# Attention 0: the product of the values with the ratio of the smoothing scales made by VectorE instead of GpSimd

## The reference, cut to what matters

```python
v = _fp8_linear_pertensor(ln_out, wv, wv_scale, v_in_scale).reshape(b, s, g, d)
core = _gqa(q, k, v).reshape(b, s, nh * d)
...
xout = _gqa(qx, kx, vx).reshape(b, s, nh * d)
cat = jnp.concatenate([core, xout], axis=-1)
catq = _div_clamp_fp8(cat, proj_smooth)
return jnp.einsum('bsi,oi->bso', catq, wproj) * (proj_in_scale * proj_w_scale)
```

## Time and profile before

| | before |
|---|---|
| median of 3 runs | 1577.19 us |
| profiled execution | 1575.72 us, span 1574.0 us |
| TensorE busy | 1366.4 us (87%) |
| VectorE busy | 1215.8 us (77%) |
| ScalarE busy | 1018.8 us (65%) |
| GpSimd busy | 853.1 us (54%) |
| mean granted TensorE clock | 0.957 |

### The profile page before, as it was taken

How to read it: one execution, slowest core, us unless ns; L and a number is a source line. 1 busy time by engine, 2 the same in 40 slices (tenths; PEclk the granted TensorE clock), 3 DMA queues, 4 the chain that set the end, 5 groups by cost and what they waited for, 6 DMA issues and landing times. The chain is left out here.

```text
span 1574.0 us, 30371 instructions
## 1 busy us (share of the span) xinstructions
PE 1366.4 (87%) x11712; PEld 1173.5 (75%) x11712; DVE 1215.8 (77%) x2318; ACT 1018.8 (65%) x2168; POOL 853.1 (54%) x912
## 2 busy tenths in 40 slices
PE   0356999999999999999999996999769898994995
PEld 0356899999999999999999985676536555553995
DVE  7999888888888888888888797633448988886554
ACT  4687677877777777778777774312136665652773
POOL 2688767667677676676775464101114433341673
PEclk9999999999999999999999998999979998995997
DMA  3100000000100000001001002340254002003563
GB/s 102 37 24 28 15 22 15 15 21 15 35 15 14 22 15 15 22 15 35 3 14 51 2 1 78 77 62 21 57 97 74 15 1 68 1 15 132 182 216 127
DMA packets 62239, 69.85 MB, mean 44 GB/s; under 512 B 5424, under 2 KB 54800, under 8 KB 61968
## 3 DMA queue, kind: packets, MB, share of 16 engines
q1 hardware_dynamic: 59488, 60.54, 14.6%
q0 software_dynamic: 2432, 7.34, 1.4%
q10 hardware_dynamic: 176, 0.04, 0.0%
HBM read 55.56 MB, written 12.34 MB: 43 GB/s over the span
## 5 line engine op out<-in xcount | busy, mean ns | idle before, releaser
L903 POOL TENSOR_TENSOR RB<-YS,M 128x512 bf16<-128x512 f32 x128 | 151.8, 1186 | 180.3 <-DVE YS L753 180.3
L579 ACT ACTIVATE QT<-B,sm 128x256 f32<-128x256 f32 x256 | 130.4, 560 | 163.8 <-PE B L435 163.8
L1769 POOL TENSOR_SCALAR_AFFINE_SELECT P<-P 128x1024 f32<-128x1024 f32 x64 | 82.1, 1282 | 154.7 <-ACT P L1623 154.7
L455 PE MATMUL SS<-QT,KT 128*128 128x256 f32 x512 | 154.8, 397 | 11.4 <-DVE mx L714 11.3
L892 POOL TENSOR_TENSOR yy<-vv,half 128x12 f32<-128x12 f32 x64 | 147.8, 2310 | 5.3
L403 PE MATMUL PA<-WH,XQ 128*128 128x256 f32 x512 | 140.2, 305 | 7.0 <-ACT SQ L608 7.0
L733 DVE TENSOR_TENSOR QN<-QN,yy 128x512 f32<-128x512 f32 x128 | 134.1, 1048 | 1.7 <-POOL yy L892 1.5
L714 DVE TENSOR_REDUCE mx<-SS 128x4 bf16<-128x512 f32 x128 | 88.2, 689 | 60.7 <-PE SS L447 59.7
L405 PE MATMUL PA<-WL,XQ 128*128 128x256 f32 x512 | 128.8, 283 | 0.0
L726 DVE TENSOR_REDUCE vv<-SQ 128x6 f32<-128x768 f32 x128 | 120.6, 942 | 0.0
L435 PE MATMUL B<-identf,QN 128*128 128x128 f32 x768 | 105.5, 274 | 6.4 <-ACT LNT L534 6.4
(11 more groups left out here) (331 smaller groups left out, 4516.1 us busy)
## 6 DMA issues: line engine op xcount, KB each, us to landing
W<-in_w SPq DMA_DIRECT2D x16, 1024.0 KB
Q<-qsc SPq DMA_DIRECT2D x48, 128.0 KB
WR<-in_wprojT SPq DMA_DIRECT2D x16, 256.0 KB, 3.0
K<-ksc SPq DMA_DIRECT2D x12, 256.0 KB
qsc<-T POOLq DMA_DIRECT2D x8, 384.0 KB, 4.2
X<-in_x SPq DMA_DIRECT2D x4, 512.0 KB, 5.9
CR<-in_xctxT SPq DMA_DIRECT2D x8, 256.0 KB, 2.8
RSM<-rsm_d SPq DMA_DIRECT2D x16, 128.0 KB, 4.1
```

Source lines behind the costliest of these rows:

```text
L455: pe.matmul(SS[:, 256 * z:256 * z + 256], k[:, 128 * z:128 * z + 128], q[:, 256 * z:256 * z + 256], start=True, stop=False)
L579: a.activation(QT[i % 2][:, o:o + 256], B1[:, o:o + 256], ACT.Identity, bias=col(n + "b"), scale=col(n + "w"))
L903: p.tensor_tensor(RB[i % 2][:], YS[:], M[:], ALU.subtract).then_inc(s_rb, 1)
```

## The change

The function `pool_values_scaled` goes, and `dve_values_scaled` takes its place, with the same operands and the same two waits. In VectorE's step it stands behind the quantisation of the output, and it is for unit `n - 2`, where GpSimd had made unit `n - 3` between the quantised inputs and `RB`.

```diff
--- before.py
+++ after.py
@@ -733,6 +733,12 @@
             v.tensor_tensor(q[:, 0:4], q[:, 0:4], y[:, 6 * h:6 * h + 4].unsqueeze(2).broadcast_to([128, 4, 128]),
                             ALU.mult).then_inc(s_mul, 1)
 
+        def dve_values_scaled(v, i):
+            v.wait_ge(s_vev, i + 1)
+            if i >= 4:
+                v.wait_ge(s_LO, i - 3)
+            v.tensor_tensor(VR1[i % 4][:, :, 0:128], V[i % 7][:, :, 0:128], RSM[i // NB % 2][:, 1], ALU.mult).then_inc(s_vq, 1)
+
         def dve_quant(v, i):
             o = PO[:, :, 0:258].rearrange("p z (j d) -> p z j d", d=129)
             v.wait_ge(s_LO, i + 1)
@@ -806,6 +812,8 @@
                     dve_quad_round(v, q4, k + 1)
                 if 0 <= n - 6 < N:
                     dve_quant(v, n - 6)
+                if 0 <= n - 2 < N:
+                    dve_values_scaled(v, n - 2)
                 for at_, g in weight_steps(n):
                     if at_ == W_CENTRE0 or at_ == W_CENTRE1:
                         dve_weights_centre(v, g, at_ == W_CENTRE1)
@@ -890,13 +898,6 @@
                 p.tensor_scalar(v_, v_, 1.0 / 128, EPS, ALU.mult, ALU.add).then_inc(*ps.up())
                 p.wait_ge(*ps.at())
                 p.tensor_tensor(yy[j % 2][:], v_, half[:], ALU.pow).then_inc(s_rstd, 1)
-
-        def pool_values_scaled(p, i):
-            g = i // NB
-            p.wait_ge(s_vev, i + 1)
-            if i >= 4:
-                p.wait_ge(s_LO, i - 3)
-            p.tensor_tensor(VR1[i % 4][:, :, 0:128], V[i % 7][:, :, 0:128], RSM[g % 2][:, 1], ALU.mult).then_inc(s_vq, 1)
 
         def pool_rounded(p, i):
             p.wait_ge(s_ys, i + 1)
@@ -930,8 +931,6 @@
                     q4, k = quad_at(n)
                     pool_quad_round(p, q4, k)
                     pool_quad_round(p, q4, k + 1)
-                if 0 <= n - 3 < N:
-                    pool_values_scaled(p, n - 3)
                 if 0 <= n - 6 < N:
                     pool_rounded(p, n - 6)
                 for at_, g in weight_steps(n):
```

## The result

| | before | changed |
|---|---|---|
| median of device time, us (16 runs each) | 1579.86 | 1572.56 |
| profiled execution: time, us | 1575.72 | 1573.67 |
| profiled execution: span, us | 1574.0 | 1571.9 |
| GpSimd busy, us (instructions) | 853.1 (912) | 776.6 (784) |
| VectorE busy, us (instructions) | 1215.8 (2318) | 1233.5 (2446) |

The ratio of the medians of paired series is 0.9949 (95% interval 0.9934 to 0.9964); of 1577.2 us that is -8.05 us, between -10.4 and -5.7. Forecast were 1569.2 us and -8.0. The median itself is 3.4 us above 1569.2, because the three runs that the forecast started from have a median of 1577.19 us and these 16 one of 1579.86; the plain difference of the two medians is -7.3 us.

What follows compares the result with a forecast made beforehand. TensorE was taken to bound the kernel from 170 to 930 us, VectorE from 80 to 170. Terms -6.4 - 1.2 - 0.4 = -8.0 us gave 1569.2 from a median of 1577.19; range 1564.0 to 1577.0.

Steps and rivals of the forecast that it cites:

- Rival B: 170 to 930 us: RB's stalls stay, waiting for something unseen; only 1.6 us gained elsewhere, 1575.6 us; chance 0.05.
- the forecast 0.44: Stalled steps: RB, started earlier, meets less of QN's product and takes 1.16 instead of 1.60 us.
- The steady term: 170 to 930 us: TensorE's six stalls for RB go, 6.4 us gained, between 4.2 and 6.6.
- 0.37 still fits: Weight-means steps: VectorE's added product costs 0.37 us and fits the 0.66 us before TensorE wants mx.
- The ceiling of 6.6: 170 to 930 us: most that could be gained, all six of TensorE's stalls for RB removed.
- The first stretch: 80 to 170 us, VectorE busy: products cost 2.6, relief 3.1 and 0.7; net -1.2 us, between +2.9 and -3.8.
- The -0.7 us for QN's product at 95.28: First stretch: without VR delaying GpSimd's reciprocal root, QN's product no longer waits 0.67 us.
- The last steps: End of the attention: RB wait of 1.07 goes, two products ahead of mx cost 0.7; net -0.4 us, -1 to +0.5.
- What was to be seen: Signs of being right: no RB waits from 170 to 930 us, VR 0.41 us before RB, GpSimd down 95, VectorE up 45.
- rival C: Each step: RB starts first and VectorE's product waits 1.16 us for it; 1612 us, slower; chance 0.09.
- the 0.3 named: 170 to 930 us: VectorE's idle time before mx was to fall by about 0.3 us a step.
- New waits for mx: Sign of being wrong: TensorE newly waits for mx after 170 us; cover gone would cost up to 5.7 us.

Runs made afterwards that it cites:

- the three profiles: The changed kernel profiled three times, each beside the kernel before; the ratios to it were 0.9949, 0.9953 and 0.9950.
- the doubled product: The changed kernel with each VR made twice on VectorE; ratio 1.0267 to the kernel before, 42 us slower.

## Why the prediction was right, and where its terms were not

**Direction and mechanism: right.** RB stood behind VR in GpSimd's queue, and that was the stall of the six steps. Rival B is refuted by every kernel that takes VR from in front of RB: the stalls went. GpSimd's side of the formerly stalled step in the changed kernel, with the DMA issue of SP, VectorE's product for QN and TensorE's restart:

```profile
461.66 0.40 POOL L879 CAST W<-WR 128x256 bf16<-128x256 f32 x1
...
462.08 0.34 SPq L321 DMA_DIRECT2D WR<-in_wqT  x1
...
466.42 4.31 POOL L853 TENSOR_SCALAR WR<-WR,csc 128x256 f32<-128x256 f32 x4 [1.79 <-DMA WR<-in_wvT]
...
470.99 2.30 POOL L900 TENSOR_TENSOR yy<-vv,half 128x12 f32<-128x12 f32 x1
473.25 1.15 POOL L904 TENSOR_TENSOR RB<-YS,M 128x512 bf16<-128x512 f32 x1
...
473.32 1.63 DVE L733 TENSOR_TENSOR QN<-QN,yy 128x512 f32<-128x512 f32 x1 [0.33 <-POOL yy L900]
...
474.46 0.40 PE L479 MATMUL PC<-identb,RB 128*128 128x128 bf16 x4 [0.16 <-POOL RB L904]
```

Against the earlier trace rows, the last cast, the loads and the scaling come as a block; the interval from the last cast to the start of the scaling is 4.76 us, 4.85 before. The prediction had RB start 0.69 us earlier. Measured from the point at which TensorE would have gone on without a wait (480.11 before, 474.30 here), RB started 0.62 us ahead of it before and 1.05 now: 0.43 gained. The scaling starts 0.45 us earlier against that point but takes 4.31 us instead of 3.61, so it ends 0.25 later, and that is taken from VR's 0.69. RB itself takes 1.15 instead of 1.60 us, 0.45 for the forecast 0.44. Together 0.88 against a stall of 1.03: 0.16 stays, six times. The step that failed is that an earlier start leaves the scaling's length alone.

**The steady term: 6.4 forecast, 4.5 by the listed waits, 2.8 to 3.2 in TensorE's time.** 5.6 of the 6.6 went, and 1.1 came back as listed waits for mx. But the time between the restarts, at like clock and without the 0.69 of the last mx, fell by 3.1, 2.8 and 3.2 us only in the three profiles. The step that failed is "0.37 still fits", in the step with weight means. VectorE and TensorE there in the changed kernel:

```profile
479.21 0.82 PE L435 MATMUL B<-identf,QN 128*128 128x128 f32 x6
479.47 0.68 DVE L714 TENSOR_REDUCE mx<-SS 128x4 bf16<-128x512 f32 x1
...
480.20 0.70 PE L455 MATMUL SS<-QT,KT 128*128 128x256 f32 x2 [0.18 <-DVE mx L714]
480.74 0.28 PE L458 MATMUL SS<-negib,mx 128*128 128x128 bf16 x2
```

mx ends at 480.15 and TensorE goes on at 480.20. I had read the slack as 0.66 us in the step of the earlier trace rows and called it the tighter one. The other weight-means step, the one right behind the stall, reads in the kernel before:

```profile
484.91 0.68 DVE L714 TENSOR_REDUCE mx<-SS 128x4 bf16<-128x512 f32 x1
...
485.88 0.82 PE L435 MATMUL B<-identf,QN 128*128 128x128 f32 x6
486.54 0.60 PE L455 MATMUL SS<-QT,KT 128*128 128x256 f32 x2
486.97 0.28 PE L458 MATMUL SS<-negib,mx 128*128 128x128 bf16 x2
```

That is 486.54 - 485.59 = 0.95 us of slack, and it looks wider; but TensorE comes there 1.03 us late because of the very stall that the change removes. The kernel with VR behind RB on GpSimd, without stall and without a product on VectorE, shows what is really there:

```profile
483.81 0.82 PE L435 MATMUL B<-identf,QN 128*128 128x128 f32 x6
483.94 0.68 DVE L714 TENSOR_REDUCE mx<-SS 128x4 bf16<-128x512 f32 x1
...
484.67 0.70 PE L455 MATMUL SS<-QT,KT 128*128 128x256 f32 x2
485.21 0.28 PE L458 MATMUL SS<-negib,mx 128*128 128x128 bf16 x2
```

TensorE goes on 0.05 us behind the end of mx (484.62), just as in the changed kernel, where this is listed as a wait: it is held here too, and the slack is nothing. Slack read behind a stall contains the stall. The bound behind the stall was there in before, and the stall hid it.

These rows also give the price. From the start of L435 to the start of L458 is 1.09 us in before, where nothing holds TensorE, 1.40 with VR behind RB and 1.53 in the changed kernel. So mx costs 0.31 us in such a step even where VectorE has no product to make, and 0.44 with it, for the 0.18 in the list. The list counts only from the end of the matmul in front (480.03), but a matmul that isn't held starts 0.16 us ahead of that end (0.66 behind the start of L435 in before, whose six take 0.82), and from L455 to L458 it then takes 0.43 and not 0.54 us. Six times 0.44 is 2.6; 5.6 - 2.6 = 3.0, which is the measured term. The ceiling of 6.6 was not to be had either: the kernel without any product has 4.9.

**The first stretch: -1.2 forecast, -2.98, -2.68 and -2.66 measured.** The cost taken by itself was right: seven products of 0.42 us, 0.34 from start to start, 2.4 (forecast 2.6). The relief was mis-sized. VectorE's groups from 93 to 167 us (count | busy, mean ns of one | idle before) before:

```profile
L679 DVE TENSOR_SCALAR QM<-QM 128x512 bf16<-128x512 bf16 x14 | 10.3, 736 | 0.0
L733 DVE TENSOR_TENSOR QN<-QN,yy 128x512 f32<-128x512 f32 x7 | 8.7, 1243 | 0.7 <-POOL yy L892 0.7
```

and in the changed kernel:

```profile
L679 DVE TENSOR_SCALAR QM<-QM 128x512 bf16<-128x512 bf16 x14 | 9.1, 653 | 0.0
L733 DVE TENSOR_TENSOR QN<-QN,yy 128x512 f32<-128x512 f32 x8 | 8.3, 1035 | 1.1 <-POOL yy L900 1.1
...
L740 DVE TENSOR_TENSOR VR<-V,RSM 128x256 f32<-128x256 f32 x7 | 2.9, 420 | 0.0
```

L679 falls from 736 to 653 ns, L733 from 1243 to 1035, the mask operation (L749, now L755) from 777 to 576, the next (L751, now L757) from 500 to 294. Over the shortest duration that each kind of instruction has in this stretch, VectorE's instructions from the mx at 93.06 to the mx at the restart together lose 23.2 us in before, and the same ones in the changed kernel 17.9: 5.3 us of relief, where I had counted 3.1 by looking only at the instruction directly beside each VR. What VR delays on GpSimd meets VectorE later as well, and I left that out. 5.3 - 2.4 = 2.9 is near the measured gain. The kernel without any product splits the same gain differently, and it is the experiment: its restart says 3.85 for the removal, and a net 0.87 and not 2.4 for the seven products. In it the same instructions lose 19.0 us, so 4.2 of the relief come from the removal and 1.1 more with the products on VectorE. Most of that is QN's product, 1160 ns there and 1035 in the changed kernel, eight of each:

```profile
L733 DVE TENSOR_TENSOR QN<-QN,yy 128x512 f32<-128x512 f32 x8 | 9.3, 1160 | 0.2 <-POOL yy L893 0.2
```

That a product set ahead of it on VectorE takes QN's product past some work of GpSimd fits this, but no row was followed for it. The Trainium skill, page "SBUF — State Buffer", section "Who interferes with whom", names VectorE instructions with two SBUF inputs and the two-port modes of single-input ones as the kinds that contend with GpSimd; the groups whose means fell are of these kinds, and the row maximum, which it counts among those that never contend, keeps its 0.68 us in both kernels.

The -0.7 us for QN's product at 95.28 did not come. GpSimd's timeline and VectorE's:

```profile
88.16 4.53 POOL L853 TENSOR_SCALAR WR<-WR,csc 128x256 f32<-128x256 f32 x4
...
92.95 2.30 POOL L900 TENSOR_TENSOR yy<-vv,half 128x12 f32<-128x12 f32 x1
...
95.28 1.65 DVE L733 TENSOR_TENSOR QN<-QN,yy 128x512 f32<-128x512 f32 x1 [1.13 <-POOL yy L900]
```

VR's 1.18 us are gone from before the scaling, and the scaling starts 0.94 us earlier, but it takes 4.53 instead of 3.58 us. The reciprocal root starts at 92.95, as before, and QN's product waits until 95.28, as before, 1.13 us now for 0.67, since VectorE is there sooner. The freed time on GpSimd went into the contention with VectorE. A relief larger by 2.2 us, a wait of 0.7 that stayed and a cost smaller by 0.2: together the term's error of -1.8 (rounded).

**The last steps: -0.4 forecast.** The mx wait grew by 0.69 (0.7 forecast) and the RB wait of 1.07 went, which shortened the way to the next restart by 0.99: -0.3. This term was right; in the first profile a drop of the clock hides it.

**The sum.** The three profiles read at like clock -3.0 - 3.1 - 0.3 = -6.4 us, -5.75 and -6.1, against -8.0 forecast and -7.4 to -8.05 measured in the ratios. The first stretch gave 1.5 to 1.8 us more than forecast and the steady steps 3.2 to 3.6 less, so the errors cancel in part: direction and range rest on the mechanism, the nearness of the number on chance. That the medians show 1 to 2 us more than the attention is open. Their intervals (5.7 to 10.4 in the first series) hold about 6 us as well, and the attention of before is known from one profile only, of an execution faster than each of the 16 runs beside the changed kernel.

**What was to be seen.** No wait for RB was forecast between 170 and 930 us: six of 0.16 us stayed. VR on VectorE takes 0.42 us and starts ahead of RB. The tile, and one step in the order of starts:

```profile
L740 DVE TENSOR_TENSOR VR<-V,RSM x128: 415/420/432, 78.7 to 937.7; 128x256 f32<-128x256 f32 x128
```

```profile
462.57 0.69 DVE L759 SCALAR_TENSOR_TENSOR YS<-Y,M 128x512 f32<-128x512 bf16 x1
463.18 0.42 DVE L740 TENSOR_TENSOR VR<-V,RSM 128x256 f32<-128x256 f32 x1
...
463.34 1.29 POOL L904 TENSOR_TENSOR RB<-YS,M 128x512 bf16<-128x512 f32 x1 [1.28 <-DVE YS L759]
```

So rival C's condition is false by 0.16 us; its price is the 42 us of the doubled product. RB pays a little for it instead, as the row of its tile shows:

```profile
L904 POOL TENSOR_TENSOR RB<-YS,M x128: 1151/1278/1289, 112.6 to 957.8; 128x512 bf16<-128x512 f32 x128
```

Its median is 1.278 us, 0.116 over the one of before (1.162). That is most of why GpSimd's busy time fell by 76.5 us and not by 95; the scaling is the other part. VectorE's rose by 17.7 and not by 45: 53.8 us of products are paid by 36 us of shorter instructions elsewhere. The idle time of VectorE before mx and X, for the earlier trace rows:

```profile
L714 DVE TENSOR_REDUCE mx<-SS 128x4 bf16<-128x512 f32 x115 | 79.1, 688 | 39.7 <-PE SS L447 38.8
L719 DVE SCALAR_TENSOR_TENSOR X<-PC,cx,X 128x256 f32<-128x256 f32 x115 | 55.4, 482 | 23.5 <-PE PC L489 22.7
```

59.1 fell to 39.7 and 29.2 to 23.5: before mx 0.17 us a step instead of the 0.3 named, with X 0.22. New waits for mx were listed among the signs of a wrong prediction; they did come, six of them, and gave back 2.6 of the 5.6 us.

## What to carry to other kernels

Ask of a slow engine's queue not only how much is in it but what stands in front of the instruction that the critical engine wants: moving VR behind RB gave as much, within the intervals, as moving it to another engine, and put no work on any other engine. Before spending slack, take away from it every stall that lies upstream in the same step: 0.95 us of slack behind a stall of 1.03 were none. Add up gains from the starts of the critical engine's instructions and not from a list of waits: a wait listed at 0.18 us delayed TensorE by 0.44. And compare single profiles only where the granted clock is the same. When two engines disturb each other, the price of an instruction depends on which of them starts first, here 0.42 or 1.27 us for the same product, 0.46 us apart in its start.

## What the runs showed of the hardware

- GpSimd and VectorE take turns in both directions. A 128x512 product of GpSimd that VectorE's 128x256 product precedes by 0.16 us takes 1.28 instead of 1.16 us; VectorE's product that starts 0.30 us behind GpSimd's takes 1.27 instead of 0.42, and at 0.51 us behind, 0.94; both end 0.3 us behind the other's end.
- Work taken from a GpSimd that shares its time with a busy VectorE does not all become free time: 1.18 us removed ahead of a scaling of 3.58 us lengthened that scaling to 4.53. GpSimd's power on 12 columns held nothing up: beside one of 2.71 us from 107.88 in before, VectorE's L677, L679 and L683 took 0.30, 0.28 and 0.69 us.
- The granted clock has drops that not every execution has: from 165 to 180 us its mean was 0.89 or 0.90 in nine of the thirteen profiles (before among them) and 1.00 in four. Such a drop is a stretch at the lower of two levels: from 168 to 171 us before was granted 0.50 and TensorE made 16 matmuls, where the changed kernel at 1.00 made 35 from 165 to 168 us; the same work behind the restart took 4.78 instead of 3.18 us. The part behind the attention, the same code in all, took 589.5 to 601.0 us, and two profiles of the same kernel differed by up to 7.4 us in span (1567.1 and 1574.5). What decides whether a drop comes is open.
- A matmul of TensorE starts before the one in front has ended: in the kernel before L455 starts 0.66 us behind a group that takes 0.82. A wait that ends in between shows as no idle time, or as less than it costs: 0 for 0.31 us, 0.18 for 0.44.
